# First attention: the turn of the relative values in quarters over four steps, with projection jobs ahead of context and output jobs

## The chip, the cores and the metric

The kernel runs on one core of a Trainium2 chip as a single launch. The metric is the device time of that launch in microseconds, lower being better. The engines are PE (matmul, with its weight loads listed as PEld), DVE, ACT, POOL and SP, which issues most of the DMAs. Times of the trace are counted from the start of the span.

## The reference, cut to what matters

Two blocks follow each other: attention plus a mixture of experts, then a second attention plus a second mixture. The change lies in the first attention only. It runs on 32 batches of 256 rows with 16 heads of 8 channels, and adds learned relative positions both to the scores and to the values:

```python
pe_k = rel_emb_k[dist]
pe_v = rel_emb_v[dist]
score = einsum('bhqd,bhkd->bhqk', q, k) + einsum('bhqd,qkd->bhqk', q, pe_k)
attn = softmax(score, axis=-1)
ctx = einsum('bhqk,bhkd->bhqd', attn, v) + einsum('bhqk,qkd->bhqd', attn, pe_v)
return ctx @ W_out + b_out
```

The term `attn * pe_v` is the "relative values". Its matmuls leave it with query and head in an order that does not fit the ordinary context, so it has to be turned before the two are added.

## The kernel before, in words

The stage is one program of steps that all engines walk through in their own order. A batch b has 8 units (UB = 8): two halves of the query rows times four groups of heads. Step s = 8b + r starts unit s. There are 32 batches of the first attention (nb) and four more (LATE) that belong to the second attention and have no relative part, so 36 in all (NB0). Below, r is the step's place in its batch, and "odd" and "even" are those of b.

PE in step s (loop from line 1234) does, in this order: the transposes of the probabilities of unit s-2 (`turn`, line 1186); the jobs of this step (`project`, line 1109); the scores of unit s+1 and the relative scores of unit s+5 (lines 1163 and 1176); the values of unit s-3 (line 1197); a part of the relative values (line 1218); and, where due, `turn_relative` (line 1150). DVE in step s adds the bias to the scores of unit s and takes the row extreme (line 1013, four times), copies the relative scores of unit s+4 out (`rel_s`, line 1021), and then does small work: moving values (`ctx_s`, `z`), the inverse sums at r = 3, the jobs' second halves, and for pairs of batches the layer norm and the routing of the second mixture. Unit s+1's scores go to the same PSUM banks as unit s's, so PE starts them only once DVE has finished both the four row passes and the `rel_s` copy. ACT in step s does one exp, a copy of transposed probabilities, two exps, another copy, the fourth exp, and last the jobs' copies (`move`, line 851).

All jobs (q, k, v, context, out, and for even or odd batches xn2T, router1, prefix) use one PSUM bank, `M_ps`. `job_list` (from line 722) names step and order. Every job waits until the job before has been moved out (`spare_free`), by ACT for q, k and xn2T, by DVE for the others.

`turn_relative(b, half)` also writes this bank, in its upper half, at steps 8b + 14 and 8b + 15, which are r = 6 and 7 of batch b+1. Each call has 32 small matmuls (64 PE instructions and as many weight loads) and waits for all jobs whose step has come: `jobs_until(UB * b + 14 + half)`. The context job of b, at r = 0 of batch b+2, then transposes the inverse sums, and DVE adds the turned values to the ordinary ones.

In odd batches, from b = 5 on, `prefix` at r = 5 gives each row its place with its expert; after that POOL scatters the rows to DRAM with eight indirect DMAs (line 844), two after each of the row passes of units 8b+5 to 8b+8.

Of the kernel before, what the change touches and what calls it, by code (L numbers as in the profile page):

```python
# [32 lines left out]
S = 256  # L33
# [28 lines left out]
def program(nc, io, nb, cap):  # L62
# [5 lines left out]
    with ctx:  # L68
# [20 lines left out]
        cview, at = {}, 0  # L89
# [505 lines left out]
        with ExitStack() as pm:  # L595
# [126 lines left out]
            for s in range(0, UB * (NB0 + 2)):  # L722
                b, r = divmod(s, UB)
                odd = b % 2 == 1
                if r == 0 and 2 <= b < NB0 + 2:
                    job_list.append((s, "context", b - 2))
                if r == 1 and b + 1 < NB0:
                    job_list.append((s, "q", b + 1))
                if r == 2 and 2 <= b < NB0 + 2:
                    job_list.append((s, "out", b - 2))  # L730
                if r == 3 and b + 1 < NB0:
                    job_list.append((s, "k", b + 1))
                if r == 4 and b + 1 < NB0:
                    job_list.append((s, "v", b + 1))
# [12 lines left out]
            STEPS = range(-8, UB * (NB0 + 1) + 3)  # L747
# [157 lines left out]
            def _(dve):  # L905
# [96 lines left out]
                for s in STEPS:  # L1002
# [85 lines left out]
                    if b >= 3 and b % 2 == 1 and p < nb // 2:  # L1088
                        if r == 3:
                            normal_stats(p)  # L1090
                        if r == 4:
                            normal_begin()
                        if r == 6:
                            newton()
                            newton()
                        if r == 7:
                            newton()
                            normal_end(p)
# [9 lines left out]
            def _(pe):  # L1108
# [41 lines left out]
                def turn_relative(b, half):  # L1150
                    pe.wait_ge(spare_free, jobs_until(UB * b + 14 + half))
                    pe.wait_ge(rel_masked, 4 * b + 4)
                    where = z[b % 2][:, :, :].rearrange("p t (g h q) -> p t g h q", g=8, q=4)
                    for t in range(2 * half, 2 * half + 2):
                        for i in range(4):
                            for j in range(4):
                                rows = slice(32 * j, 32 * j + 32)
                                at = (t * 4 + i) * 32
                                pe.matmul(M_ps[rows, S:2 * S].rearrange("p (t g q) -> p t g q", t=2, g=8)[:, :, :, 4 * t:4 * t + 4],
                                          cview["pick_head"][:, at:at + 32], where[:, :, :, 4 * i + j, :],  # L1160
                                          start=(i == 0), stop=(i == 3), skip_group_check=True)
# [72 lines left out]
                for s in STEPS:  # L1234
# [21 lines left out]
                    if r < 2 and 0 <= b < nb:  # L1256
# [689 lines left out]
```

## Time and profile before

| | us |
|---|---|
| median of 3 runs | 2600.22 (2595.81 to 2603.77) |
| the profiled execution, its own time | 2601.3 |
| its span | 2599.2 |
| the first attention's steps, first row pass of unit 0 to that of unit 287 | 451 to 1630 |

The page gives busy time as a share of the whole span. In a stage whose engines hand work round in a circle, no share reaches 100%, and what counts is which hand-over comes last. A step's length is read as the distance between the first L1013 rows of two successive units on DVE.

### The profile page before, as it was taken

How to read it: one execution, taken by the hardware profiler on the slowest of the kernel's cores; microseconds unless marked ns; L12 is line 12 of the kernel's file. 1: busy time of each engine (PE TensorE's matmuls, PEld its weight loads, DVE VectorE, ACT ScalarE, POOL GpSimd, SP SyncE). 2: the span in 40 equal slices, each digit the busy share in tenths (PEclk: the TensorE clock that was granted, in tenths of full speed). 3: DMA queues.
4: the chain of work that ended last, by engine and by line, in shares of the span. 5: the costliest groups of instructions: out<-in, count | busy, mean ns of one | idle time of the engine just before them, and what ended most of it. 6: DMA issues, size and time to landing. Idle time of an engine off the chain costs nothing. (4 is left out here: it accounts for less than half of the span.)

```text
span 2599.2 us, 86943 instructions
## 1 busy us (share of the span) xinstructions
PE 2248.8 (87%) x32420; PEld 1793.8 (69%) x32420; DVE 1927.7 (74%) x7683; ACT 1720.2 (66%) x5582; POOL 839.4 (32%) x906
## 2 busy tenths in 40 slices
PE   5999998898898898888888888799987888787888
PEld 4888886677777777777777765577775555555555
DVE  6877773787788877778878766588876767676777
ACT  2333332887677777777777778566656778777778
POOL 3566664021111111111111122212126444545451
PEclk9999998999999999999999999799998989999999
DMA  6867543776677766667767630222311110111110
GB/s 199 238 171 191 116 107 78 183 182 166 168 175 173 179 167 170 167 167 176 175 167 177 166 85 14 89 101 101 113 63 30 27 30 25 26 26 32 26 31 11
DMA packets 361046, 304.53 MB, mean 117 GB/s; under 512 B 25656, under 2 KB 329144, under 8 KB 359240
## 3 DMA queue, kind: packets, MB, share of 16 engines
q1 hardware_dynamic: 350152, 271.93, 41.2%
q0 software_dynamic: 10496, 27.28, 3.5%
q8 instruction: 252, 4.13, 0.7%
q14 instruction: 146, 1.20, 0.2%
HBM read 166.43 MB, written 132.69 MB: 115 GB/s over the span
## 5 line engine op out<-in xcount | busy, mean ns | idle before, releaser
L873 ACT ACTIVATE probs<-neg_scores,low 128x256 f32<-128x256 f32 (+1 forms) x1152 | 574.1, 501 | 147.7 <-DVE low L1013 119.3
L1013 DVE CUSTOM_DVE_ANT_0 neg_scores<-scores,rel_bias 128x256 f32<-128x256 f32 x1024 | 373.3, 421 | 186.4 <-PE scores L1182 134.8
L1773 DVE CUSTOM_DVE_ANT_0 neg_scores<-scores,alibi 128x128 f32<-128x128 f32 (+1 forms) x896 | 266.2, 353 | 129.4 <-remote 71.9
L1194 PE MATMUL probsT<-consts,probs 128*128 128x128 f32 x2240 | 321.3, 287 | 5.0 <-issue 2.7
L1172 PE MATMUL scores<-k_heads,q_heads 32*128 32x256 f32 (+1 forms) x2304 | 211.0, 432 | 101.3 <-DVE rel_s L1021 67.0
L1735 ACT ACTIVATE probs<-neg_scores,low 128x128 f32<-128x128 f32 (+1 forms) x448 | 199.8, 447 | 139.1 <-DVE low L1773 125.1
L1194 PEld LDWEIGHTS probsT<-consts,probs 128*128 128x128 f32 x2240 | 250.1, 145 | 38.2 <-issue 12.4
L889 ACT COPY probsT_s<-probsT 128x512 f32<-128x512 f32 x288 | 167.5, 582 | 151.6 <-PE probsT L1194 137.7
L295 POOL TENSOR_TENSOR hid<-hid,gate_bc 128x512 f32<-128x512 f32 x160 | 205.6, 1290 | 155.6 <-DVE hid L487 142.9
L825 POOL TENSOR_SCALAR q_heads<-q_raw,consts,q_bias 128x256 f32<-128x256 f32 x128 | 69.7, 560 | 551.2 <-ACT q_raw L856 551.1
L1021 DVE COPY rel_s<-scores 128x768 f32<-128x768 f32 x256 | 244.1, 953 | 3.9 <-DMA rel_rows<-rel_s 2.7
L324 ACT ACTIVATE ga<-gate_up 128x512 f32<-128x512 f32 x160 | 95.7, 598 | 227.2 <-PE gate_up L566 225.5
L1829 PE MATMUL scores<-rel_v 32*128 32x128 f32 (+1 forms) x1792 | 146.8, 399 | 94.1 <-DVE low L1773 80.6
L1841 PE MATMUL probsT<-consts,probs 128*128 128x128 f32 x1344 | 199.5, 287 | 23.9 <-DVE probsT_s L1781 20.9
L873 ACT ACTIVATION_READ_ACCUMULATOR probs<-neg_scores,low 128x1 f32 x1152 | 220.1, 191 | 0.0
L1172 PEld LDWEIGHTS scores<-k_heads,q_heads 32*128 32x128 f32 x2304 | 99.7, 189 | 165.3 <-issue 87.9
L1841 PEld LDWEIGHTS probsT<-consts,probs 128*128 128x128 f32 x1344 | 156.4, 147 | 62.0 <-issue 42.8
L1747 ACT ACTIVATE probs<-neg_scores,low 128x128 f32<-128x128 f32 (+1 forms) x448 | 198.5, 445 | 0.0
L1214 PE MATMUL values<-probsT_s,v_heads 128*32 128x128 f32 x4480 | 190.6, 286 | 3.7 <-issue 3.6
L1781 DVE COPY probsT_s<-probsT 128x512 f32<-128x512 f32 x224 | 154.0, 687 | 42.4 <-PE probsT L1841 25.3
L1829 PEld LDWEIGHTS scores<-rel_v 32*128 32x128 f32 x1792 | 76.5, 198 | 146.8 <-DVE low L1773 108.8
L577 PEld LDWEIGHTS ffn_down<-weights,hid 128*128 128x128 f32 x1280 | 167.1, 191 | 13.2
(227 smaller groups left out, 5132.3 us busy)
## 6 DMA issues: line engine op xcount, KB each, us to landing
rel_rows<-rel_s SPq DMA_DIRECT2D x256, 192.0 KB
rel_bias<-rel_rows SPq DMA_DIRECT2D x256, 192.0 KB, 3.4
gate_bc<-gate_rows SPq DMA_DIRECT2D x32, 1024.0 KB, 10.2
rel_rows<-rel_s SPq DMA_DIRECT2D x256, 128.0 KB
rel_bias<-rel_rows SPq DMA_DIRECT2D x256, 128.0 KB, 3.4
packed<-ffn_in SPq DMA_DIRECT2D x8, 1280.0 KB, 15.5
xe<-packed SPq DMA_DIRECT2D x16, 640.0 KB, 3.9
expert_out<-ye POOLq DMA_DIRECT2D x16, 640.0 KB, 3.2
```

The source lines that it names most:

```text
L295: pool.tensor_tensor(hid[p % 2][:, k, :], hid[p % 2][:, k, :], gate_bc[p % 2][:, min(k, NCHUNK), :], ALU.mult).then_inc(hid_done, 1)
L873: act.activation(probs[s % 3][:, j, 0:w], neg[s % 2][:, j, 0:w], ACT.Exp, bias=low[s % 3][:, j:j + 1], scale=-1.0, accum_out=sums[s // UB ...
L1013: dve.tensor_tensor_reduce(neg[s % 2][:, j, 0:w], S_ps[:, 512 * j:512 * j + w], bias_of(s)[:, j, :] if s < NU0 else alibi[:, 4 * j + s % 4 ...
L1021: dve.tensor_copy(rel_s[u % 2][:, :, :], S_ps[:, :].rearrange("p (j w) -> p j w", j=4)[:, :, S:S + 3 * R]).then_inc(rel_moved, 1)
L1172: ins = pe.matmul(S_ps[:, 512 * j:512 * j + w], q_of[b % 2][rows, i, qt * P:(qt + 1) * P], k_of[b % 2][rows, 0:w], start=True, stop=True)
L1194: ins = pe.transpose(PT_ps[kt][:, j * P:(j + 1) * P], probs[u % 3][:, j, kt * P:(kt + 1) * P], ident)
L1214: ins = pe.matmul(O_ps[rows, 0:P], v_of[b % 2][:, kt, i, rows], probsT[:, qt, i, kt, j, :], start=(i == 0 and kt == 0), stop=(i == 3 and k ...
L1735: act.activation(probs[s % 3][:, j, 0:w], neg[s % 3][:, j, 0:w], ACT.Exp, bias=low[s % 3][:, j:j + 1], scale=-1.0, accum_out=sums[g % 2][: ...
L1747: act.activation(probs[s % 3][:, j, 0:w], neg[s % 3][:, j, 0:w], ACT.Exp, bias=low[s % 3][:, j:j + 1], scale=-1.0, accum_out=sums[g % 2][: ...
L1773: dve.tensor_tensor_reduce(neg[s % 3][:, j, 0:w], S_ps[j][:, 0:w], alibi[:, 4 * j + i, S - w:S], 1.0, 3e38, ALU.add, ALU.min, low[s % 3][: ...
L1829: ins = pe.matmul(S_ps[j][:, 0:w], q_of[b % 2][rows, i, q0:q0 + P], kT[b % 2][rows, 0:w], start=True, stop=True)
L1841: ins = pe.transpose(PT_ps[kt][:, j * P:(j + 1) * P], probs[u % 3][:, j, kt * P:(kt + 1) * P], ident)
```

## The change

Three edits.

1. `turn_relative` takes a quarter t of the work (16 matmuls, 32 PE instructions) and is called in four successive steps, 8b + 14 to 8b + 17, so at r = 6 and 7 of batch b+1 and r = 0 and 1 of batch b+2. It still waits for all jobs up to its own step.
2. In a batch the jobs run q (r = 0), k (1), context (2), v (3), out (4), where they ran context (0), q (1), out (2), k (3), v (4). The other jobs stay. The step loop is two steps longer, since the last context and output jobs are later.
3. On DVE, in odd batches, the statistics of the layer norm go from r = 3 to r = 4, and their first evaluation from r = 4 to r = 6.

```diff
-                if r == 0 and 2 <= b < NB0 + 2:
+                if r == 0 and b + 1 < NB0:
+                    job_list.append((s, "q", b + 1))
+                if r == 1 and b + 1 < NB0:
+                    job_list.append((s, "k", b + 1))
+                if r == 2 and 2 <= b < NB0 + 2:
                     job_list.append((s, "context", b - 2))
-                if r == 1 and b + 1 < NB0:
-                    job_list.append((s, "q", b + 1))
-                if r == 2 and 2 <= b < NB0 + 2:
+                if r == 3 and b + 1 < NB0:
+                    job_list.append((s, "v", b + 1))
+                if r == 4 and 2 <= b < NB0 + 2:
                     job_list.append((s, "out", b - 2))
-                if r == 3 and b + 1 < NB0:
-                    job_list.append((s, "k", b + 1))
-                if r == 4 and b + 1 < NB0:
-                    job_list.append((s, "v", b + 1))
...
-            STEPS = range(-8, UB * (NB0 + 1) + 3)
+            STEPS = range(-8, UB * (NB0 + 1) + 5)
...
-                        if r == 3:
+                        if r == 4:
                             normal_stats(p)
-                        if r == 4:
+                        if r == 6:
                             normal_begin()
-                        if r == 6:
                             newton()
                             newton()
...
-                def turn_relative(b, half):
-                    pe.wait_ge(spare_free, jobs_until(UB * b + 14 + half))
+                def turn_relative(b, t):
+                    pe.wait_ge(spare_free, jobs_until(UB * b + 14 + t))
...
-                    for t in range(2 * half, 2 * half + 2):
...
-                    if r < 2 and 0 <= b < nb:
+                    if r < 4 and 0 <= b < nb:
                         turn_relative(b, r)
```

## Rows read from the trace of the kernel before

**Rows 1.** The page, busy us and share of the span:

```profile
PE 2248.8 (87%) x32420; PEld 1793.8 (69%) x32420; DVE 1927.7 (74%) x7683; ACT 1720.2 (66%) x5582; POOL 839.4 (32%) x906
```

**Rows 2.** Timeline, batch 15, r = 0 to 2: start us, us, engine, line:

```profile
947.53 0.42 DVE L1013 CUSTOM_DVE_ANT_0 neg_scores<-scores,rel_bias 128x256 f32<-128x256 f32 x1 [0.61 <-ACT probs L873]
...
947.94 0.97 PEld L1159 LDWEIGHTS projected<-z,consts 128*32 128x32 f32 x64
...
949.00 0.85 PEld L1194 LDWEIGHTS probsT<-consts,probs 128*128 128x128 f32 x8
...
950.24 0.31 PEld L1172 LDWEIGHTS scores<-k_heads,q_heads 32*128 32x128 f32 x8 [0.17 <-issue]
...
951.35 0.42 DVE L1013 CUSTOM_DVE_ANT_0 neg_scores<-scores,rel_bias 128x256 f32<-128x256 f32 x1
...
952.23 0.86 PEld L1194 LDWEIGHTS probsT<-consts,probs 128*128 128x128 f32 x8
...
952.93 0.59 ACT L889 COPY probsT_s<-probsT 128x512 f32<-128x512 f32 x1 [0.19 <-PE probsT L1194]
...
953.80 0.34 PEld L1172 LDWEIGHTS scores<-k_heads,q_heads 32*128 32x128 f32 x8 [0.45 <-issue]
...
954.93 0.42 DVE L1013 CUSTOM_DVE_ANT_0 neg_scores<-scores,rel_bias 128x256 f32<-128x256 f32 x1 [1.24 <-PE scores L1182]
...
955.16 0.57 PEld L1229 LDWEIGHTS values<-probsT_s,rel_v 128*32 128x32 f32 x32
...
955.37 0.37 ACT L856 COPY q_raw<-projected 128x256 f32<-128x256 f32 x1
...
955.82 0.86 PEld L1194 LDWEIGHTS probsT<-consts,probs 128*128 128x128 f32 x8
```

**Rows 3.** Groups by line, 450 to 1650 us: busy us, mean ns:

```profile
L860 ACT ACTIVATE k_heads<-projected,weights 128x256 f32<-128x256 f32 x31 | 14.4, 463 | 0.0
```

**Rows 4.** Timeline of DVE, batch 15, r = 3 and 4:

```profile
958.60 0.42 DVE L1013 CUSTOM_DVE_ANT_0 neg_scores<-scores,rel_bias 128x256 f32<-128x256 f32 x1 [0.68 <-DVE residual L1080]
...
961.64 0.87 DVE L918 BATCH_NORM_STATS2 stats<-residual 128x6 f32<-128x128 f32 x4
...
962.54 0.42 DVE L1013 CUSTOM_DVE_ANT_0 neg_scores<-scores,rel_bias 128x256 f32<-128x256 f32 x1
...
965.12 0.48 DVE L1063 TENSOR_TENSOR v_heads<-projected,rows 128x128 f32<-128x128 f32 x2
965.52 0.37 DVE L923 BATCH_NORM_AGGREGATE mv<-stats 128x2 f32<-128x6 f32 x4
...
966.55 0.42 DVE L1013 CUSTOM_DVE_ANT_0 neg_scores<-scores,rel_bias 128x256 f32<-128x256 f32 x1
```

**Rows 5.** Timeline of PE's weight loads, batch 13, r = 7, during the scatter:

```profile
907.99 0.30 PEld L1159 LDWEIGHTS projected<-z,consts 128*32 128x32 f32 x13 [1.49 <-issue]
...
911.18 1.09 PEld L1159 LDWEIGHTS projected<-z,consts 128*32 128x32 f32 x39 [0.58 <-issue]
912.44 1.57 PEld L1194 LDWEIGHTS probsT<-consts,probs 128*128 128x128 f32 x8 [0.17 <-issue]
```

**Rows 6.** Timeline of POOL: scatters that waited for a row pass (wait in brackets):

```profile
641.84 0.96 POOL L844 DMA_INDIRECT packed<-xn,scat  x1 [8.32 <-DVE low L1013]
...
908.23 0.96 POOL L844 DMA_INDIRECT packed<-xn,scat  x1 [1.41 <-DVE low L1013]
918.02 0.96 POOL L844 DMA_INDIRECT packed<-xn,scat  x1 [7.57 <-DVE low L1013]
...
1189.39 0.96 POOL L844 DMA_INDIRECT packed<-xn,scat  x1 [2.98 <-DVE low L1013]
1194.12 0.96 POOL L844 DMA_INDIRECT packed<-xn,scat  x1 [2.51 <-DVE low L1013]
...
1467.83 0.96 POOL L844 DMA_INDIRECT packed<-xn,scat  x1 [7.14 <-DVE low L1013]
```

**Rows 7.** Timeline of DVE, batch 13: the row pass that begins r = 7:

```profile
906.49 0.42 DVE L1013 CUSTOM_DVE_ANT_0 neg_scores<-scores,rel_bias 128x256 f32<-128x256 f32 x1 [0.86 <-remote]
```

More of the change, by code:

```diff
@@ L1148, in project @@
                     ins.then_inc(spare_full, 1)
-                def turn_relative(b, half):
-                    pe.wait_ge(spare_free, jobs_until(UB * b + 14 + half))
+                def turn_relative(b, t):
+                    pe.wait_ge(spare_free, jobs_until(UB * b + 14 + t))
                     pe.wait_ge(rel_masked, 4 * b + 4)
                     where = z[b % 2][:, :, :].rearrange("p t (g h q) -> p t g h q", g=8, q=4)
-                    for t in range(2 * half, 2 * half + 2):
[L1155 to L1161, printed above, removed]
+                    for i in range(4):
+                        for j in range(4):
+                            rows = slice(32 * j, 32 * j + 32)
+                            at = (t * 4 + i) * 32
+                            pe.matmul(M_ps[rows, S:2 * S].rearrange("p (t g q) -> p t g q", t=2, g=8)[:, :, :, 4 * t:4 * t + 4],
+                                      cview["pick_head"][:, at:at + 32], where[:, :, :, 4 * i + j, :],
+                                      start=(i == 0), stop=(i == 3), skip_group_check=True)
                 def score(u):
```

## The prediction, made blind

> **What bounds the kernel now.** The page comes first. No engine is full: PE is busy 87% of the span, DVE 74%, ACT 66% [rows 1]. So the limit is a circle of hand-overs, and the timeline is read next, step by step, in the first steps of a batch, which no scatter disturbs. The circle of a plain step is the one from 951.35 to 954.93: DVE starts its row passes at 951.35, PE starts the next scores at 953.80, 2.45 us later, and DVE starts the next passes 1.13 us after that: 3.58 us [rows 2]. The reader is to see that PE's own work does not set this: it had a gap of 0.45 us ahead of the scores, and DVE waited 1.24 us for them. PE has some slack per step, and so has DVE behind the `rel_s` copy. A change pays only where a step is longer than 3.58.
>
> Two kinds of steps are. First, steps that carry too much. At r = 0 of an odd batch the turn's 64 instructions, the transposes and the context job together reach the scores at 950.24, which is 2.71 after 947.53; the step lasts 3.82 [rows 2]. At r = 3 DVE is the later one: 958.60 to 962.54 is 3.94, because the statistics take 0.87; at r = 4 it is 4.01 [rows 4].
>
> Second, and larger, the scatter. While POOL issues its indirect DMAs, PE moves in small groups of instructions with "issue" gaps between. In batch 13 the turn gets 13 loads through at 907.99 and its last 39 only from 911.18, where the disturbance ends; the transposes behind it start at 912.44 [rows 5]. The seventh scatter's wait tells how long the row pass of the next unit took: 8.32 and 7.14 us in the first and the last of 8 "long" batches (641.84, 1467.83), but 2.51 at 1194.12, which stands for 5 "short" ones [rows 6]. Batch 31, whose scatters wait for less, has gaps like the 8, so I count 9 long ones.
>
> **The change, part by part.** All durations are of the profiled execution, 2601.3 us, which is 1.1 above the median.
>
> *r = 0, odd.* One quarter of 32 instructions stands here in place of a half of 64, and q in place of context. From the turn's first load to the transposes it took 949.00 - 947.94 = 1.06; 0.43 of that goes, half of the time in which 64 loads are issued [rows 2]. The scores could start at 2.71 - 0.43 = 2.28, so the 2.45 of the plain circle holds: 3.58, a gain of 0.24. q and context are two weight loads each, and I take them as equal.
>
> *r = 1 and 2: the added wait.* The third quarter, on PE at the end of step r = 0, waits for `spare_free` of q, the job of that same step, and ACT copies q at the very end of its step. The fourth waits likewise for k. Behind the waiting PE instruction stand the transposes of the next step, behind these ACT's copies and exps, and behind these ACT's next job copy: lateness is passed on once. The round is priced from the rows: transposes to ACT's first copy 952.93 - 952.23 = 0.70; from there over the exps to the q copy 955.37 - 952.93 = 2.44; the copy 0.37 (k: 463 ns, rows 3); then a quarter and its hand-over to the transposes, 1.06 - 0.43 = 0.63, and 0.05 for the semaphore [rows 2, 3]. Together 4.2 for q and 4.3 for k, against a step of 3.58. Now follow it. In r = 0 the transposes start at 949.00 - 0.43 - 947.53 = 1.04. In r = 1 they start at 1.04 + 4.2 - 3.58 = 1.65; without the wait it would be 955.82 - 954.93 + 0.43 = 1.32. From transposes to scores it is 950.24 - 949.00 = 1.24, and from scores to the next step 1.11, so the step lasts 1.65 + 1.24 + 1.11 = 4.00: plus 0.42. In r = 2 they start at 1.65 + 4.3 - 4.00 = 1.95 and the step lasts 4.30 where it lasted 3.67 (954.93 to 958.60): plus 0.6 [rows 2, 4]. No row of before shows this wait, so its bounds are no wait at all, where PE's added quarter alone costs 0.13 and 0.06 in the two steps, and the full round, 0.42 and 0.6. I take the round, because the q copy at 955.37 to 955.74 lies only just before the place where a third quarter would stand, between the relative values and the transposes at 955.82 [rows 2].
>
> *The Trainium skill on this wait.* The wait could look needless, since the quarter writes the upper half of the bank and the copy reads the lower. The Trainium skill's page "PSUM — Partial Sum Buffer", section "PSUM bank collisions raise a hardware error", says that accesses are to be guarded by bank, not by address. No row here shows a collision; the rule changes no term, it only says why the wait must be paid where it falls.
>
> *r = 3 and 4, odd.* At r = 3 the statistics (0.87) go and the two v moves (0.48, less their overlap) come: the small work starts its last part at 961.64, 3.04 after 958.60, so the step ends at about 3.69, minus 0.25. At r = 4 v and the first evaluation (from 965.52 to 966.55, 1.0) go, and out and the statistics come: about 3.89 against 4.01, minus 0.12 [rows 4]. *r = 6, odd.* The first evaluation, 1.0, comes to the longest small work of DVE. DVE had slack there, because PE was held by the scatter: it waited 0.86 at 906.49 [rows 7]. So plus 0.14, between 0 (where the wait is longer) and 1.0 (where the wait is gone). An odd batch then changes by -0.24 + 0.42 + 0.6 - 0.25 - 0.12 + 0.14 = +0.55.
>
> *Even batches.* r = 0 comes after the scatter's last two DMAs and stays as it is. ACT is early there, so q's wait is covered at r = 1: 0. k's wait is not: r = 2 plus 0.4, between 0.07 (DVE's `z` and context in one step) and 0.6. At r = 3 DVE gets v: plus 0.1. At r = 7 minus 0.05. Sum +0.45.
>
> Fifteen odd and fifteen even batches from b = 3 to 32 give 15 x (0.55 + 0.45) = +15. Batches 2 and 3 have no scatter ahead of them and PE's load at r = 0 goes down there too; I book -1. So **+14 us** of calm steps.
>
> *The scatter.* In a long batch the turn at r = 6 has 32 instructions where it had 64. Before, 25 were through when the disturbance ended at 911.18, and the other 39 and the transposes came after, 912.44 - 911.18 = 1.26 later [rows 5]. Now about 7 are left at 911.18, and the transposes start some 1.1 earlier. What comes before 911.18 gives nothing, since POOL's DMAs set it. 9 x 1.1 = **-10 us**.
>
> *At nothing:* POOL gets q one step earlier and idles before it anyway. SP's queue is unchanged. Two more steps at the end are empty; the last values, context and output still follow one another, with the same instructions.
>
> Sum: 2601.3 + 14 - 10 = 2605.3. Against the median of before, 1.1 lower: **2604**.
>
> **The rivals.**
>
> *Slower: the round is paid in full and the scatter takes the gain back.* The place is the same window. If PE, with fewer turns to do, meets the scores or the transposes inside the disturbance and still leaves it at the same time, or if POOL's DMAs simply come later because r = 6 is longer by DVE's 1.0, the -10 falls away: 2601.3 + 14 - 1 = 2614. It decides from the point where the transposes do not start earlier than 1.26 after the gaps end. For it: the first and last of the eight long waits are of one size, so POOL may set them. Against it: the 39 loads after 911.18 are real time [rows 5]. Chance 0.25; the full 1.0 at r = 6, 0.86 more in 9 batches, would add up to 8.
>
> *Faster: the long batches become short ones.* The gap ahead of the turn ends at 907.99, and the fifth scatter starts at 908.23 [rows 5, 6]. Thirty-two instructions need 0.5 us; if the longer r = 6 delays the fifth scatter by that much, the turn slips through. A long batch then saves (7.57 - 2.51) - (2.98 - 1.41) = 3.5 [rows 6]: 9 x 3.5 = 31, so 2601 + 14 - 31 - 1 = 2583. Against it: the delay is only 0.14 by my sum. Chance 0.12.
>
> *Faster: the wait is covered.* If ACT's copies come as early as they do now relative to PE, odd batches change by -0.24 + 0.13 + 0.06 - 0.25 - 0.12 + 0.14 = -0.28 and even ones by +0.1: 15 x -0.18 = -3, then -1 and -10, and 1.1 for the median: 2586. The rows speak against it, by the round of 4.2. Chance 0.12.
>
> *Faster: the gaps are a supply limit by count.* If instructions come to PE at a fixed rate there, 32 fewer save (911.18 - 907.99) / 25 x 32 = 4.1 each [rows 5]: 9 x 4.1 = 37, giving 2601 + 14 - 37 - 1 = 2577. The sudden end of the gaps, after which 39 loads pass at once, speaks against it. Chance 0.04. The Trainium skill, "Runtime: NRT & Kernel Launch", section "Instruction fetch mechanics", says that sequential fetch is hidden, which would rule this out; rows 5 have the gaps all the same.
>
> *That it doesn't do what it says* can hardly be: the calls and waits are fixed in the program.
>
> **How the numbers follow.** Forecast (2604): 0.47; the slower rival (2614): 0.25; the three faster ones (2583, 2586, 2577): 0.28. A measurement of this kernel tells about 0.3% from no change, 7.8 us, so faster means below 2592 and slower above 2608. The forecast's own spread is about 5 us each way, from r = 2 and r = 6, and a small part of it lies above 2608. That gives faster 0.26, same 0.44, slower 0.30. The range takes in the slower rival and part of the faster ones: 2584 to 2618. The forecast's own range is 2597 to 2611.
>
> **What would show it.** Right: in odd batches r = 0 is 3.58, r = 1 about 4.0, r = 2 about 4.3, with PE waiting for ACT's L856 and L860 ahead of L1159; r = 3 is 3.7; and in long batches the transposes follow the end of the gaps at once. Wrong: if r = 1 and r = 2 stay near 3.7, the wait is covered and the time falls below 2592; if the seventh scatter's waits are all 2.5, the long batches are gone; if r = 6 grows to 6 or more without r = 7 shrinking, the time goes to 2614 and above.

## The result and the profile after

The changed kernel took 2575.41 us (median of 4, 2568.63 to 2581.08) against 2601.99 (median of 4, 2595.81 to 2617.08) for the kernel before, measured side by side: ratio 0.9888, 95% interval 0.9839 to 0.9937. It is 1.1% faster, 28.6 us below the forecast of 2604 and 8.6 below the low end of the range. The time is near that of two rivals, the one in which the long batches become short (2583) and the supply limit by count (2577); the trace tells which.

The page after, in answer to [rows 1]; the profiled execution took 2576.7 us:

```profile
span 2575.1 us, 86977 instructions
...
PE 2238.4 (87%) x32420; PEld 1786.6 (69%) x32420; DVE 1933.6 (75%) x7683; ACT 1715.5 (67%) x5582; POOL 837.5 (33%) x906
```

The shares tell nothing of the change. (PE's lines are two lower in the changed kernel: L1157 is the turn, L1170 and L1180 the scores, L1192 the transposes.) The waits of PE between 451 and 1650 us do tell (us in total, times, longest): before, after.

```profile
PE projected L1159 <- issue: 28.8, 52, 1.3
```

```profile
PE projected L1157 <- issue: 5.4, 13, 0.5
```

Most of the turn's "issue" gaps are gone; those of its weight loads, in the same view, fell from 39.8 to 16.8 us. The time that POOL's scatters wait for a row pass fell by 30 us, from 98.2 to 67.9 (in a group's row, behind the bar: idle time before these instructions and what ended it), before and after:

```profile
L844 POOL DMA_INDIRECT packed<-xn,scat x128 | 124.9, 975 | 132.9 <-DVE low L1013 98.2 <-issue 26.0 <-POOL scat L818 8.7
```

```profile
L844 POOL DMA_INDIRECT packed<-xn,scat x128 | 124.7, 975 | 101.6 <-DVE low L1013 67.9 <-issue 25.0 <-POOL scat L818 8.7
```

Between batches 5 and 29 no seventh scatter waits longer than 3.28 us; before, eight waited 6.48 to 8.32 [rows 6].

The medians of the step lengths, as distances between first L1013 rows, over the odd batches 5 to 29; the last two lines belong to runs explained below:

| us | r=0 | 1 | 2 | 3 | 4 | 5 | 6 | 7 |
|---|---|---|---|---|---|---|---|---|
| before | 3.82 | 3.58 | 3.67 | 3.94 | 4.01 | 4.74 | 5.60 | 8.76 |
| forecast | 3.58 | 4.00 | 4.30 | 3.69 | 3.89 | 4.74 | +0.14 | |
| after | 3.59 | 4.14 | 4.02 | 3.58 | 3.94 | 4.74 | 6.42 | 4.80 |
| e3b, near to before, no gaps | 3.82 | 3.58 | 3.68 | 3.94 | 4.01 | 4.74 | 4.79 | 4.06 |
| a3, the changed kernel, no gaps | 3.59 | 4.14 | 4.02 | 3.58 | 3.93 | 4.74 | 6.04 | 4.07 |

Summed over those 13 batches, after less before, r = 7 gives -35.9 us; r = 1 and 2 cost 7.2 and 5.0, r = 6 3.9, r = 0, 3 and 4 give back 3.5, 4.7 and 0.9. That is -28.9. The even batches 6 to 30 cost 4.6. The rest of the 24.1 us between the spans is small: batch 31 -1.7, batches 0 to 4 with the start +3.8, batches 32 to 35 +5.4, and -7.4 behind the last step, of which 4.8 lie in the unchanged second attention. All of the gain is in one step of 13 batches.

That step in the changed kernel, batch 15 (which had been long before): timeline of DVE, PE's loads and POOL, r = 6 from 964.33, r = 7 from 970.36:

```profile
964.33 0.42 DVE L1013 CUSTOM_DVE_ANT_0 neg_scores<-scores,rel_bias 128x256 f32<-128x256 f32 x1
...
970.36 0.42 DVE L1013 CUSTOM_DVE_ANT_0 neg_scores<-scores,rel_bias 128x256 f32<-128x256 f32 x1
...
971.32 0.57 PEld L1157 LDWEIGHTS projected<-z,consts 128*32 128x32 f32 x32 [1.40 <-issue]
971.98 0.86 PEld L1192 LDWEIGHTS probsT<-consts,probs 128*128 128x128 f32 x8
...
972.11 0.97 POOL L844 DMA_INDIRECT packed<-xn,scat  x1 [1.83 <-DVE low L1013]
...
973.00 0.31 PEld L1170 LDWEIGHTS scores<-k_heads,q_heads 32*128 32x128 f32 x8 [0.17 <-issue]
...
975.20 0.42 DVE L1013 CUSTOM_DVE_ANT_0 neg_scores<-scores,rel_bias 128x256 f32<-128x256 f32 x1 [0.69 <-PE scores L1180]
```

The gaps that the first four scatters bring end at 971.32, 6.99 us after the step r = 6 began; in batch 13 of before it was 907.99 - 900.90 = 7.09, nearly the same. The fifth scatter starts 7.78 after it (972.11); before, it started 7.33 after it (908.23, [rows 6]). Between the end of one disturbance and the start of the next scatter there were 0.24 us before, in which 13 of 64 loads went through [rows 5], and there are 0.79 now, in which all 32 loads pass and the transposes have begun. Little of PE's path is left for the second disturbance to hold: r = 7 lasts 4.84 us here, and 4.06 or 4.07 in most batches of the runs without gaps.

In these two batches the clock adds to it. The windows view (length, busy us and number of each engine, then PEclk, the granted clock) of r = 7, first in batch 13 of before, then in batch 15 of after:

```profile
908.00:911.18 3.18, 1.62 (x25) 0.88 (x25) 0.82 (x1) 0.00 (x0) 1.92 (x2) 0.69 0.45 116
911.18:913.00 1.82, 1.81 (x42) 1.65 (x43) 1.58 (x8) 0.00 (x0) 0.00 (x0) 0.50 0.93 206
```

```profile
971.32:973.00 1.68, 1.68 (x41) 1.43 (x40) 1.65 (x7) 0.49 (x3) 0.89 (x1) 1.00 0.37 104
973.00:975.20 2.20, 1.85 (x43) 1.47 (x46) 1.44 (x6) 2.20 (x8) 1.04 (x2) 1.00 0.59 140
```

Before, PE was busy for 1.62 of 3.18 us among the gaps, and the clock was at 0.50, the level of 1.2 GHz, when the 39 loads and the transposes came; the 8 transpose loads took 1.57 us [rows 5]. After, they took 0.86 at a clock of 1.00, the level of 2.4 GHz.

That is no condition of the gain. In eight of the 13 odd batches of the changed kernel the mean clock of r = 7 was 0.56 to 0.70, and the step lasted 4.72 to 5.50 us all the same. Batch 29, where it was lowest:

```profile
1439.76:1445.27 5.51, 4.49 (x64) 3.65 (x67) 4.04 (x18) 1.30 (x4) 1.92 (x2) 0.56 0.61 149
```

### The profile page after: what moved, and what is told of

It is laid out like the page before. It is cut to its first block and busy times, and to the rows that moved or that the text cites. A ratio compares the mean times of both kernels' runs of the same rounds, so it can differ in the third digit from the quotient of the medians.

```text
span 2575.1 us, 86977 instructions
## 1 busy us (share of the span) xinstructions
PE 2238.4 (87%) x32420; PEld 1786.6 (69%) x32420; DVE 1933.6 (75%) x7683; ACT 1715.5 (67%) x5582; POOL 837.5 (33%) x906
## 5 line engine op out<-in xcount | busy, mean ns | idle before, releaser
L1013 DVE CUSTOM_DVE_ANT_0 neg_scores<-scores,rel_bias 128x256 f32<-128x256 f32 x1024 | 373.2, 421 | 174.6 <-PE scores L1180 143.8
L1192 PE MATMUL probsT<-consts,probs 128*128 128x128 f32 x2240 | 322.5, 288 | 5.7 <-ACT probsT_s L889 2.7
L1170 PE MATMUL scores<-k_heads,q_heads 32*128 32x256 f32 (+1 forms) x2304 | 212.0, 436 | 96.0 <-DVE rel_s L1021 53.3
L1192 PEld LDWEIGHTS probsT<-consts,probs 128*128 128x128 f32 x2240 | 250.9, 145 | 38.1 <-issue 12.2
L1170 PEld LDWEIGHTS scores<-k_heads,q_heads 32*128 32x128 f32 x2304 | 99.3, 192 | 158.9 <-DVE low L1013 84.2
L1779 DVE COPY probsT_s<-probsT 128x512 f32<-128x512 f32 x224 | 153.9, 687 | 43.4 <-PE probsT L1839 26.5
```

Of the source, the lines that this page charges most:

```text
L1013: dve.tensor_tensor_reduce(neg[s % 2][:, j, 0:w], S_ps[:, 512 * j:512 * j + w], bias_of(s)[:, j, :] if s < NU0 else alibi[:, 4 * j + s % 4 ...
L1170: ins = pe.matmul(S_ps[:, 512 * j:512 * j + w], q_of[b % 2][rows, i, qt * P:(qt + 1) * P], k_of[b % 2][rows, 0:w], start=True, stop=True)
L1192: ins = pe.transpose(PT_ps[kt][:, j * P:(j + 1) * P], probs[u % 3][:, j, kt * P:(kt + 1) * P], ident)
L1779: dve.tensor_copy(probsT[u % 3][:, 0, :, :].rearrange("p g q -> p (g q)"), PT_ps[0][:, :]).then_inc(moved0, 1)
```

## The experiments

**Two conditions.** One fact governs all that follows. The kernels ran in groups, each on one chip with the kernel before beside it. In some groups the kernel before took 2599 to 2603 us as at first, in others 2385 to 2387, with the same program. All kernels of one group shared one condition. One chip gave before at 2598.5 in one group and at 2385.2 in a later one, so it does not belong to the chip alone. In the lower condition the scatter's "issue" gaps are all but absent, and the unchanged second attention takes 524 to 526 us instead of 623 to 639. I call them "with gaps" and "without gaps". The expectations of the first group (e1, e2, e3, e4) were written for the one with gaps, before I knew of the other.

| kernel | with gaps: us, ratio to before | without gaps |
|---|---|---|
| changed kernel (first result) | 2575.4, 0.9888 [0.9839, 0.9937] | |
| changed kernel (a1, a2; a3) | 2569.2, 0.9877 [0.9819, 0.9935]; 2569.2, 0.9894 [0.9858, 0.9930] | 2430.6, 1.0173 [1.0149, 1.0196] |
| changed, first evaluation at r = 4 (e2b; e2) | 2604.0, 1.0028 [1.0007, 1.0048] | 2422.2, 1.0149 [1.0132, 1.0166] |
| before, first evaluation at r = 6 (e7) | 2579.7, 0.9936 [0.9899, 0.9972] | |
| before with edit 3 alone (e1, e1b, e1c) | | 2404.8, 2405.7, 2404.6: 1.0079 to 1.0086 |
| changed, turn in halves (e4, e4b, e4c, a4, e4d) | | 2408.0 to 2411.5: 1.0091 to 1.0106 |
| before, fifth scatter a step later (e3, e3b) | | 2386.2, 2384.5: 0.9994, 0.9992 |
| changed, early copies of q and k (e5; e5b) | 2559.3, 0.9835 [0.9777, 0.9893] | 2420.0, 1.0140 [1.0123, 1.0157] |

**Edit 3 alone.** In the kernel before, the statistics go to r = 4 and the first evaluation to r = 6.

```diff
-                        if r == 3:
+                        if r == 4:
                             normal_stats(p)
-                        if r == 4:
+                        if r == 6:
                             normal_begin()
-                        if r == 6:
```

> The kernel before with the third edit alone: in odd batches DVE's statistics go from r = 3 to r = 4 and the first evaluation from r = 4 to r = 6. The turn stays in two halves, the jobs where they were. Theory A (the gain is timing: DVE's longer r = 6 holds back the row pass that POOL's fifth scatter waits for, so the turn passes between the fourth and the fifth): r = 6 is 6.0 us or more in every odd batch with a scatter, r = 7 falls to about 4.8 to 5.3 in all of them, the seventh scatter's wait is 2.5 everywhere, and with 0.4 less at r = 3 and 4 the time is about 2565. Theory B (the gain is the smaller turn: only 32 instructions fit into the gap): r = 7 stays near 9 in about 8 batches and the time is near 2600.

> The kernel before with the layer norm's move alone, once more, since the first run fell on a chip without the gaps. On a chip where the kernel before takes about 2600 us. Theory A (DVE's longer r = 6 holds the fifth scatter back until the turn has passed): r = 7 is 4.7 to 5.4 us in every odd batch, and the time is about 2602 - 25 - 5 = 2572. Theory B (only the smaller turn fits into the gap): r = 7 is 8 to 10 in most batches, the time 2590 to 2600. On a chip without the gaps: 2405 against 2387, as before.

> The kernel before with the layer norm's move alone. On a chip with the gaps (before near 2600). Theory A (DVE's longer r = 6 is enough): r = 7 at most 5.5 in all odd batches, about 2572. Theory AB (both are needed: at a 6.0 us long r = 6 some 0.4 to 0.5 us are left between the end of one disturbance and the start of the next, enough for 32 turn instructions and not for 64): r = 7 is short only where r = 6 took 6.4 or more, and 6.5 to 9 elsewhere; the time is 2580 to 2600. On a chip without gaps: 2405 against 2387, as twice before.

All three fell without gaps, where the edit costs 17.5 to 19.6 us. Against e3b, r = 6 goes from 4.79 to 6.05, r = 3 from 3.94 to 3.58, r = 4 from 4.01 to 3.87. On its own, without gaps, the edit only loses. With gaps it was not met.

**The first evaluation back at r = 4, all else changed.**

```diff
                         if r == 4:
                             normal_stats(p)
-                        if r == 6:
                             normal_begin()
+                        if r == 6:
                             newton()
```

> The kernel after, but the first evaluation of the layer norm runs at r = 4 behind the statistics and not at r = 6. Both theories: r = 4 grows by about 0.9 us in 15 odd batches, plus 13. Theory A: r = 6 falls to 5.6 in part of the batches, and there r = 7 grows by 2.5 to 4; the time is about 2605 to 2615. Theory B: r = 6 falls to 5.6, r = 7 stays at 4.8, about 2585.

> The kernel after with the first evaluation at r = 4 behind the statistics, so r = 6 is short again. On a chip with the gaps, theory A: r = 6 falls to 5.6 and r = 7 grows to 8 or more in part of the batches, time 2600 to 2612. Theory B (the smaller turn is what fits): r = 7 stays at 5, about 2585. On a chip without the gaps: 2422 against 2387, as before.

With gaps (e2b) the time is back at 2604.0, 34.8 us above the changed kernel in the same group. Not all of that is the scatter's. In the traces of the two (e2b less a2, over the 13 odd batches and the even ones behind them) the longer r = 4 costs 13.5 us, for it lasts 4.98 instead of 3.94; r = 6 and 7 together cost 16.0, and r = 1 of the even batches 5.1. The turn is in quarters there as well, and still 5 of its 13 odd batches are long: r = 7 is 6.6 to 8.8 us where r = 6 was 5.5 or 5.6. In 7 others r = 6 was 6.4 or more, and r = 7 at most 4.8; one lies between, 5.8 and 5.8. PE's waits give the turn about half of its gaps back:

```profile
PE projected L1157 <- issue: 15.7, 30, 1.2
```

One of the long ones, timeline of batch 11, r = 6 from 840.29:

```profile
845.80 0.42 DVE L1013 CUSTOM_DVE_ANT_0 neg_scores<-scores,rel_bias 128x256 f32<-128x256 f32 x1 [0.78 <-remote]
...
847.32 0.43 PEld L1157 LDWEIGHTS projected<-z,consts 128*32 128x32 f32 x11 [1.45 <-issue]
...
847.55 0.97 POOL L844 DMA_INDIRECT packed<-xn,scat  x1 [1.30 <-DVE low L1013]
...
850.50 0.25 PEld L1157 LDWEIGHTS projected<-z,consts 128*32 128x32 f32 x8 [0.54 <-issue]
850.92 1.57 PEld L1192 LDWEIGHTS probsT<-consts,probs 128*128 128x128 f32 x8 [0.17 <-issue]
...
854.32 0.42 DVE L1013 CUSTOM_DVE_ANT_0 neg_scores<-scores,rel_bias 128x256 f32<-128x256 f32 x1 [1.77 <-PE scores L1180]
```

The first gaps end 847.32 - 840.29 = 7.03 us after the step began, as in the kernels before and after. But the fifth scatter starts 7.26 after it, 0.23 us later, and cuts the turn after 11 loads; the transposes come at 850.92. So DVE's longer r = 6, which holds back the row pass and with it the fifth scatter, is needed for all odd batches to be short. It is not needed for the whole gain: against the kernel before, r = 6 and 7 of the 13 batches are still 17.3 us shorter in e2b, where they are 32.1 shorter in the changed kernel. There are fewer long batches, 5 where there were 8, which one trace of each cannot tell from chance, and r = 6 and 7 of the long ones take 12.1 to 14.3 us, 13.6 in the mean, where they took 15.0. The supply limit by count is hard to keep as the cause: e2b has no more instructions of the turn at r = 6 than the changed kernel, the long ones save 1.4 and not the 4.1 of that rival, and where the turn falls between two disturbances all its 32 loads pass in 0.57 us.

Without gaps (e2) the steps are r = 4 4.98 instead of 3.93 and r = 6 4.80 instead of 6.04. The first evaluation costs about as much in one place as in the other; the time is 8 us less than a3's, of another group.

**The first evaluation at r = 6, alone.** In the kernel before, only `normal_begin()` moves from r = 4 to r = 6; the turn stays in halves and the jobs in their order.

```diff
-                        if r == 4:
-                            normal_begin()
                         if r == 6:
+                            normal_begin()
                             newton()
```

> The kernel before; only the first evaluation of the layer norm moves from r = 4 to r = 6 of the odd batches, the statistics stay at r = 3. On a chip with the gaps, theory A: r = 6 is 6.0 or more, r = 7 short in all odd batches, minus 20 to 30. Theory B: r = 7 stays near 9 in most. On a chip without the gaps: r = 6 from 4.8 to 6.05, r = 4 from 4.0 to 3.6: plus 12.

With gaps, 2579.7 us, against 2598.5 of before and 2569.2 of the changed kernel in that group. So moving one small piece of DVE work into the longest step gives back 19 us. Some 6 of them have nothing to do with the scatter: r = 4 falls from 4.01 to 3.58. The six executions spread widely, from 2567.0 to 2607.1 us, and the trace is of the last of these, well above the median, so the counts of its batches need not be its usual ones. In it r = 6 is 6.0 us or more in every odd batch, as in the changed kernel, but r = 7 is 6.6 to 8.9 in ten of the 13; only where r = 6 was 6.4 was r = 7 4.9 to 5.8. One batch shows what the halves do, r = 6 from 695.35, r = 7 from 701.40:

```profile
702.38 1.60 PEld L1158 LDWEIGHTS projected<-z,consts 128*32 128x32 f32 x58 [0.59 <-issue]
...
703.14 0.97 POOL L844 DMA_INDIRECT packed<-xn,scat  x1 [1.84 <-DVE low L1013]
...
706.24 1.57 PEld L1193 LDWEIGHTS probsT<-consts,probs 128*128 128x128 f32 x8 [0.72 <-issue]
...
711.13 1.47 PEld L1158 LDWEIGHTS projected<-z,consts 128*32 128x32 f32 x54
...
711.83 0.97 POOL L844 DMA_INDIRECT packed<-xn,scat  x1 [6.44 <-DVE low L1013]
```

The turn starts at 7.03 and the scatter at 7.79, the window of the changed kernel. Of 64 loads 58 pass in one go; the last five come in two groups at 704.46 and 705.31, the transposes at 706.24, and r = 7 lasts 8.69. But 58 loads took 1.60 us here, at a granted clock of 0.50, where 64 took 0.97 at [rows 2]. Whether a half would slip through at the full clock this row does not tell. The clock alone does not explain the ten, though: in four of them its mean over r = 7 was 0.65 to 0.69 and the step lasted 6.6 to 7.1, while the changed kernel's r = 7 lasted at most 5.5 at 0.56 to 0.58.

The halves are caught a second time. The other half of the turn, from 711.13, meets the seventh scatter at 711.83, its last ten loads come in three small groups until 714.91, and r = 0 of the even batch lasts 7.26. Behind those ten batches r = 0 took 7.2 to 8.9 us, where the kernel before had 4.8 in most: 28.6 us over the 13. In the changed kernel it was at most 5.1.

**The turn in halves again, all else changed.** `turn_relative` gets its inner loop over two quarters back and is called at r = 6 and 7 alone.

```diff
-                def turn_relative(b, t):
-                    pe.wait_ge(spare_free, jobs_until(UB * b + 14 + t))
+                def turn_relative(b, half):
+                    pe.wait_ge(spare_free, jobs_until(UB * b + 14 + half))
...
+                    for t in range(2 * half, 2 * half + 2):
...
-                    if r < 4 and 0 <= b < nb:
+                    if r < 2 and 0 <= b < nb:
```

> The kernel after, but the turn is made in two halves at r = 6 and 7 as before, so PE waits for no job copy of ACT at r = 0 and 1. Theory A: r = 7 stays short (5.3 at most), r = 1 and 2 of the odd batches fall from 4.14 and 4.02 to 3.58 and 3.7, r = 0 rises to 3.8, and the time is about 2560 to 2568, below the kernel after. Theory B: the long r = 7 steps come back, about 2590 to 2600.

> The kernel after with the turn in two halves at r = 6 and 7. On a chip with the gaps, theory A: r = 7 is short in all odd batches (up to 5.4), r = 1 and 2 fall to 3.58 and r = 0 rises to 4.0 and 4.9, so the time is 2565 to 2575, that of the kernel after or a little less. Theory B: r = 7 is long again in most batches and the time is 2590 to 2600.

> The kernel after with the turn in halves at r = 6 and 7. On a chip with the gaps. Theory A: r = 7 at most 5.5, about 2565 to 2570. Theory AB: r = 7 is 6.5 to 9 wherever r = 6 took 6.0 to 6.1, and the time is 2585 to 2605, so 15 to 35 above the kernel after. On a chip without gaps: 2410 against 2387, as twice before.

> The kernel after with the turn in halves at r = 6 and 7. On a chip with the gaps (before near 2600). Theory A (DVE's longer r = 6 is enough): r = 7 at most 5.5, time about 2565 to 2570. Theory AB (the time left between two disturbances is enough for 32 turn instructions and not for 64): r = 7 is 6.5 to 9 where r = 6 took 6.0 to 6.1, and the time is 2585 to 2605. On a chip without gaps: 2410 against 2386, for the fourth time.

> The changed kernel with the turn of the relative values in halves of 64 instructions at r = 6 and 7 again, all else as changed. If the gaps of the scatter are there (before at about 2600): the theory that DVE's longer r = 6 alone makes the long batches short expects r = 7 of at most 5.5 us in all odd batches and a time of about 2575 or less; the theory that it needs both, the delay of the fifth scatter and only 32 instructions of the turn, expects r = 7 of 7 us or more where r = 6 stays at 6.0, as in the look at the kernel with the first evaluation alone moved, and a time of 2585 to 2615. If the gaps are not there: 2409, as before, and nothing is told apart.

This would have told whether the quarters are needed as well. All five fell without gaps, so it is not shown. What they do give is the price of the quarters there: 2430.6 for the changed kernel against 2408 to 2411, some 20 us, at r = 1 and 2 (3.58 and 3.58 against 4.14 and 4.02 in odd batches, 3.58 and 3.58 against 3.90 and 4.02 in even ones), less 0.44 at r = 0 of odd batches. The job order, edit 2, is left with 2 to 7 us, the distance of e4 from e1 on the same chip.

**The changed kernel again.**

> The kernel after, unchanged, beside the kernel before. The four runs before this one were on a chip whose traces show no gaps in PE during the scatter: r = 6 and 7 of the odd batches took 4.8 and 4.06 us there, and the kernel before took 2387 us. Theory C (the whole gain was the scatter's gaps; the change itself costs time): where r = 7 of the kernel before is short, the kernel after is slower, by 0.45 to 0.6 per batch at r = 1 and 2 and by 1.2 at r = 6: about plus 25 us. Theory D (the change gains also without the gaps): faster or equal there. On a chip with the gaps both expect about 25 us less than the kernel before.

> The kernel after, unchanged, a third time. If this falls on a chip without the gaps (the kernel before near 2386 us), theory C says it is slower than before by about 25 us, since it has the cost at r = 1, 2 and 6 and nothing to gain; theory D says equal or faster. On a chip with the gaps: minus 25 to 33 once more.

> The kernel after, unchanged. On a chip without the gaps it should be slower than before. From the steps of the other runs there: r = 1 plus 0.56, r = 2 plus 0.35, r = 6 plus 1.25, less 0.24 at r = 0, 0.36 at r = 3 and 0.07 at r = 4, so plus 1.5 in each odd batch, and plus 0.5 to 0.6 in each even one: 15 x 2.05 = 31 and some 3 more at the end, 2387 + 34 = 2421, between 2412 and 2424. On a chip with the gaps: 2569 against 2600, as twice before.

With gaps it repeats: 0.9877 and 0.9894 beside 0.9888, and r = 7 of batches 5 to 29 is at most 5.5 us in all three traces, 39 batches. Without gaps it is 1.7% slower. The page and the timeline of a3, batch 15, r = 6 from 957.43:

```profile
span 2430.3 us, 86977 instructions
```

```profile
961.51 0.52 PEld L1157 LDWEIGHTS projected<-z,consts 128*32 128x32 f32 x32
962.12 0.86 PEld L1192 LDWEIGHTS probsT<-consts,probs 128*128 128x128 f32 x8
...
963.47 0.42 DVE L1013 CUSTOM_DVE_ANT_0 neg_scores<-scores,rel_bias 128x256 f32<-128x256 f32 x1
...
965.21 0.97 POOL L844 DMA_INDIRECT packed<-xn,scat  x1 [1.84 <-DVE low L1013]
...
967.84 0.43 DVE L1013 CUSTOM_DVE_ANT_0 neg_scores<-scores,rel_bias 128x256 f32<-128x256 f32 x1 [0.23 <-PE scores L1180]
```

The turn stands at 4.08 after the step's start and not at 6.99, with four scatters going on beside it and no gap ahead of it. The turn and the transposes' loads are done by 962.98, before DVE ends r = 6. There is nothing to win at r = 7, which e3b, so near to the kernel before, passes in 4.06, and every added term is paid.

**The fifth scatter a step later, in the kernel before.**

```diff
-                                pool.wait_ge(lowest, 4 * min(NU0, UB * b + 6 + i))
+                                pool.wait_ge(lowest, 4 * min(NU0, UB * b + 6 + i + (i >= 2)))
```

> The kernel before; only POOL waits longer: the fifth to eighth scatter of a batch wait for the row pass of one unit later each. Theory A: the long r = 7 steps are gone, since nothing disturbs PE while the turn passes; minus 20 to 30, less what the later scatters cost in r = 0 and 1 of the even batch: 2575 to 2590. Theory B: the gap is not what held the turn; the time stays within 2595 to 2605.

> The kernel before; the fifth to eighth scatter of a batch wait for one more row pass each. On a chip with the gaps, theory A: r = 7 is short in all odd batches, about 4.1 to 4.8, and some of it comes back in r = 0 and 1 of the even batch, where four scatters now fall: 2570 to 2585. Theory B: 2595 to 2605. On a chip without the gaps: no change, as before.

This was to delay the scatter with nothing else moved. Both runs fell without gaps and changed nothing (0.9994 [0.9984, 1.0003], 0.9992 [0.9982, 1.0002]). They say nothing of the theory, but their traces stand in for the kernel before without gaps, of which there is no trace.

**A change of the wait.** In the changed kernel ACT copies q and k out ahead of the step's fourth exp.

```diff
+                    for name, b in jobs_at.get(s, ()):
+                        if name in ("q", "k"):
+                            move(name, b)
...
-                        move(name, b)
+                        if name not in ("q", "k"):
+                            move(name, b)
```

> The kernel after, but ACT copies q and k out ahead of the step's fourth exp and not behind it. If the third and fourth quarters wait for these copies, r = 1 of the odd batches falls from 4.14 to about 3.7 and r = 2 from 4.02 to about 3.8, in even batches r = 2 falls from 3.9 to 3.7, together 10 to 15 us less than the kernel after. If PE's own work sets those steps, nothing changes within 3 us.

> The changed kernel with ACT's copies of q and k moved ahead of its fourth exp. If the instruction gaps of the scatter are there (the kernel before at about 2600): 2557 to 2563 us, ratio 0.984, since it repeats. If they are not there (before at 2386): the wait of the quarters at r = 1 and r = 2 shrinks by 0.2 and 0.3 us in odd batches and 0.3 in even ones, so 15 x 0.8 = 12 less than the changed kernel's 2430.6, which is 2419.

The median is 9.9 us lower with gaps (2559.3 against 2569.2 in the same group, where the two kernels' executions just meet at 2562) and 10.7 without (2420.0 against 2430.6 of another group). With gaps it is the fastest kernel of the study, 1.65% below before; without gaps it is still 1.4% slower than before. Batch 15, r = 1 from 938.78; the lines are four higher than in the changed kernel:

```profile
938.78 0.42 DVE L1017 CUSTOM_DVE_ANT_0 neg_scores<-scores,rel_bias 128x256 f32<-128x256 f32 x1 [0.92 <-PE scores L1184]
...
938.85 0.38 ACT L856 COPY q_raw<-projected 128x256 f32<-128x256 f32 x1
...
939.50 0.52 PEld L1161 LDWEIGHTS projected<-z,consts 128*32 128x32 f32 x32
...
941.57 0.31 PEld L1174 LDWEIGHTS scores<-k_heads,q_heads 32*128 32x128 f32 x8 [0.33 <-issue]
...
942.68 0.42 DVE L1017 CUSTOM_DVE_ANT_0 neg_scores<-scores,rel_bias 128x256 f32<-128x256 f32 x1 [1.56 <-PE scores L1184]
```

The copy is over at 939.23, the turn no longer waits for it, and the step lasts 3.90 instead of 4.14; r = 2 lasts 3.68 instead of 4.02.

## Why the prediction was wrong, point by point

**The steps r = 0, 3 and 4 of odd batches** went as reckoned: 3.59 (3.58 forecast), 3.58 (3.69) and 3.94 (3.89).

**The added wait** was paid, as said, and the rival in which it is covered falls. The changed kernel's r = 0 to 2 in batch 15, the answer to [rows 2]:

```profile
940.33 0.42 DVE L1013 CUSTOM_DVE_ANT_0 neg_scores<-scores,rel_bias 128x256 f32<-128x256 f32 x1 [0.61 <-ACT probs L873]
...
942.81 0.32 PEld L1170 LDWEIGHTS scores<-k_heads,q_heads 32*128 32x128 f32 x8 [0.33 <-issue]
...
943.92 0.42 DVE L1013 CUSTOM_DVE_ANT_0 neg_scores<-scores,rel_bias 128x256 f32<-128x256 f32 x1 [0.92 <-PE scores L1180]
...
944.49 0.36 ACT L856 COPY q_raw<-projected 128x256 f32<-128x256 f32 x1
...
944.90 0.49 PEld L1157 LDWEIGHTS projected<-z,consts 128*32 128x32 f32 x32 [0.19 <-ACT q_raw L856]
...
946.95 0.31 PEld L1170 LDWEIGHTS scores<-k_heads,q_heads 32*128 32x128 f32 x8 [0.33 <-issue]
...
948.05 0.43 DVE L1013 CUSTOM_DVE_ANT_0 neg_scores<-scores,rel_bias 128x256 f32<-128x256 f32 x1 [1.80 <-PE scores L1180]
...
948.63 0.46 ACT L860 ACTIVATE k_heads<-projected,weights 128x256 f32<-128x256 f32 x1
949.14 0.49 PEld L1157 LDWEIGHTS projected<-z,consts 128*32 128x32 f32 x32 [0.30 <-ACT k_heads L860]
...
952.08 0.42 DVE L1013 CUSTOM_DVE_ANT_0 neg_scores<-scores,rel_bias 128x256 f32<-128x256 f32 x1
```

At r = 0 the scores start 942.81 - 940.33 = 2.48 after the step, the plain circle's 2.45. At r = 1 PE's turn waits for the q copy and the scores start 3.03 after. Its terms were off in both directions: +0.56 at r = 1 where 0.42 was forecast, +0.35 at r = 2 where 0.6 was. The two together are 0.91 against 1.02. My lower bound, 0.13 for PE's own work at r = 1, was too low: in e5, whose turn does not wait for ACT, the step still costs 3.90 - 3.58 = 0.32. Nor do its 0.13 and 0.06 follow from the rows given: 1.32 + 1.24 + 1.11 is 3.67, which is 0.09 more than 3.58 and no more than the 3.67 of r = 2. In even batches r = 1 cost nothing, as forecast, r = 2 0.22 (0.4 forecast), r = 3 nothing (0.1), r = 4 0.09. For the calm steps of 15 odd and 15 even batches the forecast was +14; r = 0 to 4 of the odd batches 5 to 29 came to 3.2 (forecast 0.41 each, 5.3), the even ones to 4.6 (5.9). The share that I left out lies in batches 32 to 35, which have q and k jobs up to batch 34 and quarters up to r = 1 of batch 33: +5.4, of which only 0.45 was booked, for batch 32.

**The failed step is "r = 6, odd".** I wrote that the first evaluation is 1.0 us and goes mostly into DVE's slack, "so plus 0.14". Two terms of it were mis-sized. The work is 1.23 us, not 1.0: in the changed kernel it delays the first L930, of the evaluation's next part, from 903.48 - 903.15 = 0.33 behind the start of `z` (batch 13, before) to 968.14 - 966.58 = 1.56 (batch 15, after). The 1.0 was read at r = 4, where the next row pass starts before its last instruction has ended [rows 4]. And DVE's own work filled 4.80 us of that step, as the steps without gaps show (4.79), so the step cannot be shorter than 4.80 + 1.23 = 6.03. The shortest in the changed kernel are 6.0. Against the 5.59 of a long batch that is 0.44 and not 0.14. This is a plain sum over DVE's instructions of a step, which I had not made: I took DVE's wait of 0.86 off one batch [rows 7] and subtracted. DVE at r = 6, before and after:

```profile
900.90 0.42 DVE L1013 CUSTOM_DVE_ANT_0 neg_scores<-scores,rel_bias 128x256 f32<-128x256 f32 x1
...
903.15 0.41 DVE L1038 TENSOR_TENSOR z<-values,consts 128x256 f32<-128x256 f32 x1
903.48 0.15 DVE L930 TENSOR_TENSOR nw<-nw 128x4 f32<-128x4 f32 x1
```

```profile
966.58 0.41 DVE L1038 TENSOR_TENSOR z<-values,consts 128x256 f32<-128x256 f32 x1
966.91 0.37 DVE L923 BATCH_NORM_AGGREGATE mv<-stats 128x2 f32<-128x6 f32 x4
...
968.14 0.16 DVE L930 TENSOR_TENSOR nw<-nw 128x4 f32<-128x4 f32 x1
```

**From the size to the wrong side.** I had the mechanism, as the rival with 2583 us, and dismissed it: "Thirty-two instructions need 0.5 us; if the longer r = 6 delays the fifth scatter by that much, the turn slips through", with the reason against it that "the delay is only 0.14". The fifth scatter went from 7.33 to 7.78 after the start of the step, 0.45 later, as the 0.44 says. The 3.5 us per batch were right to 0.2: the pair r = 6 and 7 took 14.3 to 15.5 us, 15.0 in the mean, in the eight long batches before, and takes 10.8 to 11.9, 11.3 in the mean, now. The sum of both steps over the 13 batches is 35.9 - 3.9 = 32.0. The ninth, batch 31, which I had counted with them, stayed long, 12.6 to 9.2 us at r = 7, and gave 1.7 as a whole. With that rival's 31 in the place of the 10, the same sum gives 2583; of the 8 us from there to 2575.4, 7.4 lie behind the last step, most of them in the second attention, which the change does not touch and which took 623 to 639 us in the traces with gaps.

**The -10 of the scatter** supposed that PE leaves the window at the same time with fewer loads to do. In the changed kernel it does not: it is through before the window opens. In e2b's long batches, where it is still caught, 1.4 us each are saved where I had put 1.1.

**The slower rival** (2614) is what happens without gaps, by another mechanism than I gave. DVE's 1.23 us have no slack to go into there. Its bounds, "0 where the wait is longer, 1.0 where the wait is gone", were the right thought. The steps of a3 less those of e3b, as means over the 13 batches, are +1.22 at r = 6, +0.58, +0.34, -0.36 and -0.07 at r = 1 to 4 in odd ones, and +0.43, +0.41 and +0.37 at r = 0 to 2 in even ones: 25.0 and 17.7 us of the 43.4 between the spans. There q's wait is not covered in even batches, as I had it from batches that a scatter had delayed.

**The wait by bank, and the gaps.** The Trainium skill's page "PSUM — Partial Sum Buffer", section "PSUM bank collisions raise a hardware error", was the reason to expect that the wait is kept. PE does wait there, 0.19 us for q and 0.30 for k in batch 15, since the program says so; no run here leaves the wait out. The Trainium skill's page "Runtime: NRT & Kernel Launch", section "Instruction fetch mechanics", says that sequential fetch is hidden. Without gaps the trace agrees (PE's matmuls of the turn have no "issue" wait in a3, its weight loads one of 0.2 us); with gaps it shows 28.8 us of them in the kernel before, and what causes them no run here tells.

**Left open.** How much of the gain DVE's delay would bring alone, with the turn in halves. For: e7 gains 19 us, some 13 of them not at r = 4. Against: in e7's one trace, of its slowest execution, r = 6 and 7 save only 4 us over the 13 batches, and r = 0 behind them loses 28.6. With what e2b shows, both the delay and the quarters seem to be needed for the full gain, but with gaps no run has the changed kernel with halves. Open too is what puts a group of runs in the one condition or the other. This change is worth 1.1% with gaps and costs 1.7% without.

## What to carry to other kernels

Where two engines meet in a window of a few tenths of a microsecond, add up each engine's instructions over the whole step ahead of it, instead of taking a wait off its end; here a delay put at 0.14 us that was 0.45 stood between the forecast and the 3.1 to 4.2 us that each of the eight long batches saved at r = 6 and 7. A delay on an engine with slack is no cost by itself: ask which transfer it triggers, and whether coming later makes that miss something. And before a gain is called one of the kernel, time it against the kernel before on several chips and occasions: this one has its sign from the condition of the run.

## What the runs showed of the hardware

The same program took 2385 or 2600 us. What the traces of the longer condition have and the others have not is instructions of PE that come late ("issue"), or hand-overs that do, while POOL runs indirect DMAs. PE's granted clock is lower too, 0.945 to 0.963 over the span with gaps and 0.973 to 0.984 without; no run tells which of the two brings the other, or whether both have one cause. The difference is largest in the second attention, which has such DMAs all along (L1647, 96.5 us of POOL in the last 625). DVE's row passes there, a group of the lines view from 1950 us to the end, with gaps (the changed kernel) and without (a3):

```profile
L1771 DVE CUSTOM_DVE_ANT_0 neg_scores<-scores,alibi 128x256 f32<-128x256 f32 (+1 forms) x874 | 260.2, 353 | 115.3 <-remote 71.5 <-PE scores L1827 39.3 <-issue 3.9
```

```profile
L1771 DVE CUSTOM_DVE_ANT_0 neg_scores<-scores,alibi 128x256 f32<-128x256 f32 (+1 forms) x810 | 241.0, 353 | 31.5 <-PE scores L1827 28.2 <-issue 0.2
```

The two stretches do not hold the same number of passes (874 and 810), so they are compared by the pass. One takes 353 ns in both; the idle time ahead of it is 0.13 us in the mean with gaps and 0.04 without, and 71.5 us of it ended with a release that the profile calls "remote", of which the run without gaps names none. The indirect DMAs themselves are not slower: 0.97 us each in either (972.11, 965.21).
